# Experts stage: choices' transposes and sends two steps behind the scores, back half ten steps behind, norms one batch less ahead

## The chip, the cores and the metric

The kernel runs on one core of one Trainium2 chip. The metric is the device time of one execution in microseconds (us); lower is better. Engines are called PE (TensorE), DVE (VectorE), ACT (ScalarE), POOL (GpSimd) and SP (SyncE, which only issues DMAs here).

## The reference, cut to what matters

Two blocks (L0, L1) of attention and feed-forward run over x of 32 batches x 256 tokens x 128. The change touches the feed-forward of L0, a mixture of experts, and the modulated norm ahead of it:

```python
h = _layernorm(x, axis=-1) * (1 + cb) + sb
x = x + gb * _L0_ffn_ref(h, ...)

# _L0_ffn_ref: x (B, L, d); t = 32 experts, 4 sets, 32 hidden
grouped = x.reshape(B, g, t, d)                      # groups of 32 tokens
logits = jnp.einsum('bgtd,des->bgtes', grouped, controller)
logits = logits + tie
perm = (logits == jnp.max(logits, axis=-3, keepdims=True)).astype(x.dtype)
dispatched = jnp.einsum('bgtd,bgtes->bgesd', grouped, perm)
inner = jax.nn.relu(jnp.einsum('bgesd,desf->bgesf', dispatched, f1) + bias)
intermediate = jnp.einsum('bgesf,esfd->bgesd', inner, f2)
out = jnp.einsum('bgesd,bgtes->bgtd', intermediate, perm)
```

In each group of 32 tokens every pair of expert and set (128 slots) takes the token with the highest score, runs it through a small two-layer network, and hands the result back to that token.

## The kernel before

The stage is `experts_0`. Each engine has one program, written out by hand as a loop over steps i = 0, 1, 2, ...; engines meet through semaphores (`wait(engine, semaphore, count)`), and each engine takes its instructions strictly in the order written. So the place of a call in the loop of an engine is its place in the queue.

**Front half**, one batch n (256 tokens) at a time. DVE: `centre(n)` computes the statistics of X (L1345 stats, L1353 moments) and writes `centred` (L1359); POOL: `root(n)` turns the variance into `rstd` (L1302, L1306); DVE: `modulate(n)` writes `h` (L1369). PE: `turn(i)` transposes h of batch i into bank 0 (L1054), and into the other half of that bank the choice `takenT` of a former batch (L1060), and ACT copies both together to SBUF (`front_out`, L1238, tile `hT_taken`). PE: `score(i)` multiplies h by the controller and adds the tie row (L1071, L1072). DVE: `choose(i)` takes the maximum of each group (L1380, `best`) and compares (L1383, `takenT`). PE: `send` gathers the chosen tokens with the transposed choice (L1084; in the steps of `HALVED` it is two halves, L1099), and ACT copies them to the slots (`sent_out`, L1250).

**Back half**, a chunk m of 8 batches (`CB_` = 8) at a time, spread over eight steps s = 0 to 7; `back(i)` gives (m, s) from i - LAG. s = 0, 1: first matrices on PE (L1114), bias on DVE (L1390), relu on ACT (L1256). s = 2, 3: second matrices on PE (L1141), four rounds in a chunk, copied by DVE and ACT (`results_out`, L1221). s = 4 to 7 (`QUARTERS`): transposes back (L1153), copies (L1228), `hand_back` (L1165), `gate` on DVE (L1398, tile `delta`), residual on POOL (L1310). In steps LAG to 31 both halves run in the same step; the last chunk's back half runs without a front half.

**Sundries.** SP loads the modulation rows of a batch (L1020, tile `e_mod_norm`, four buffers), each load after the one before has landed and after h of the batch three earlier is written. Beside the stage, pieces of the last stage's weights are rounded on ACT (L1262), compared on POOL (L1315) and summed on ACT (L1267). `keep_busy` (L72) issues matmuls into an unused bank whose results nobody reads (filler).

In a step, PE's order is: `turn`, the odd `hand_back` of the step before, first or second matrices or two transposes back, `score`, `send`, then the rest of the back half with the even `hand_back`. ACT's order is: `front_out`, pieces, relu or copies, `sent_out`. DVE's order is: gate, bias or copies, `modulate`, `choose`, more copies, `centre`.

Of the kernel before, what the change touches and what calls it, by code (L numbers as in the profile page):

```python
# [23 lines left out]
P = 128  # L24
# [902 lines left out]
def experts_0(nc, ctx, dram, sbuf, psum, following):  # L927
# [56 lines left out]
    LAG = CB_ + 1  # L984
# [16 lines left out]
    HALVED = [i for i in range(STEPS) if front(i - 1) and back(i)[1] in (2, 3)]  # L1001
# [11 lines left out]
    with nc.Block() as block:  # L1013
# [33 lines left out]
        def _(pe):  # L1047
            def turn(i):
# [6 lines left out]
                if front(i - 1):  # L1055
                    if i >= LAG and back(i)[1] not in QUARTERS:
                        keep_busy(nc, B_TAKEN, sbuf["ident16"], 3)
                    wait(pe, takenT_done, i)
                    for t in range(TT):
                        last = nc.tensor.transpose(B_TAKEN[:, t * P:(t + 1) * P], takenT[:, (i - 1) % (2 * CB_), t * P:(t + 1) * P],  # L1060
                                                   ident[:, :])
# [26 lines left out]
            def send_half(i, half):  # L1088

                wait(pe, turned_done, i + 1)  # L1090
                wait(pe, sent_done, i - 1)
                if half == 1:
                    wait(pe, half_psum, HALVED.index(i) + 1)
                n = i - 1
# [23 lines left out]
            def second_matrices(i, m, r):  # L1118

                alone = m == NCHUNK - 1  # L1120
                if r == 0:
                    if alone:
                        keep_busy(nc, bank[4], sbuf["ident16"], 5)
                    wait(pe, sent_done, min(i - 1, B))
# [5 lines left out]
                if alone and r == 1:  # L1130
                    wait(pe, turned_done, B + 1)
# [40 lines left out]
            for i in range(STEPS):  # L1172
                m, s = back(i)
                before, at = back(i - 1)
                if i <= B:
                    turn(i)
# [26 lines left out]
                if front(i - 1) and i not in HALVED:  # L1203
                    send(i)
# [26 lines left out]
        def _(act):  # L1231
            def front_out(i):
# [3 lines left out]
                wait(act, sent_psum, i - 2)  # L1236
                part = slice(0 if front(i) else T, 2 * T if front(i - 1) else T)
                nc.scalar.copy(hT_taken[i % 2][:, part], bank[0][:, part]).then_inc(turned_done, 1)  # L1238

            def sent_out(n):  # L1240
# [3 lines left out]
                if n + 1 in HALVED:  # L1244
# [25 lines left out]
            def check_pieces(i):  # L1270
                if 0 <= i - PIECE_LAG - 2 < len(pieces):
                    sum_piece(i - PIECE_LAG - 2)
                if 0 <= i - PIECE_LAG - 1 < len(pieces):
                    round_piece(i - PIECE_LAG - 1)

            for i in range(STEPS):
                m, s = back(i)
                if i <= B:
                    front_out(i)
# [11 lines left out]
                if front(i - 1):  # L1291
                    sent_out(i - 1)
# [6 lines left out]
        def _(pool):  # L1299
# [18 lines left out]
            for n in range(3):  # L1318
                root(n)
            for i in range(STEPS):  # L1320
# [6 lines left out]
                if front(i + 3):  # L1327
                    root(i + 3)
# [7 lines left out]
                if 0 <= i - PIECE_LAG - 1 < len(pieces):  # L1336
                    compare_piece(i - PIECE_LAG - 1)

        @block.vector
        def _(dve):  # L1340
# [64 lines left out]
            for n in range(2):  # L1405
                modulate(n)
                centre(n + 1)
            for i in range(STEPS):
# [11 lines left out]
                if front(i + 2):  # L1420
# [1761 lines left out]
```

## Time and profile before

| | us |
|---|---|
| median of 3 runs | 1328.28 |
| lowest, highest | 1327.71, 1328.93 |
| the profiled execution, its own time | 1332.12 |
| its span in the profile | 1330.2 |
| mean granted clock of PE, share of full | 0.962 |

| engine | busy us | share of the span | instructions |
|---|---|---|---|
| PE, matmul | 1226.8 | 92% | 13717 |
| PE, weight load | 815.6 | 61% | 13717 |
| DVE | 1059.1 | 80% | 2967 |
| ACT | 931.9 | 70% | 1338 |
| POOL | 539.0 | 41% | 760 |

How to read it: these are averages over stages with different limits. The experts stage lies between about 408 and 632 us of the span; what a change in it is worth is read from its own steps. Times in the rows below are us from the start of the span.

### The profile page before, as it was taken

To read this page: it belongs to the slowest core of one execution; us is meant where nothing else is said; L and a number is where in the kernel's file an instruction comes from. 1 tells how busy PE (TensorE), PEld (TensorE's weight loads), DVE (VectorE), ACT (ScalarE), POOL (GpSimd) and SP (SyncE) were. 2 spreads that over 40 slices of the span, in tenths; PEclk is the share of its full clock that TensorE was granted. 3 is DMA by queue.
4 is the path that set the end of the run, shared out by engine and by line. 5 is a ranking of instruction groups with operands and counts; after the bars stand their busy time and mean duration, and the time that the engine had idled before them with its cause. 6 is when DMAs were issued, how large, how long until landed. Compare 5 with 4: busy or idle time off the path is not lost. (4 is left out here: it accounts for less than half of the span.)

```text
span 1330.2 us, 39845 instructions
## 1 busy us (share of the span) xinstructions
PE 1226.8 (92%) x13717; PEld 815.6 (61%) x13717; DVE 1059.1 (80%) x2967; ACT 931.9 (70%) x1338; POOL 539.0 (41%) x760
## 2 busy tenths in 40 slices
PE   3899999999996889998899999999879999999998
PEld 1555555555543667766455555555458878778776
DVE  4799999999965787756799999999646777777763
ACT  0588888888892556542588888788637676767665
POOL 2333333433421243422343343333236565656653
PEclk6699999999998999997899999999969999999999
DMA  4311111111001222100200000000000000000000
GB/s 119 136 36 36 35 35 35 35 35 35 28 10 48 59 50 63 53 19 2 104 14 16 13 12 16 12 12 16 6 2 9 9 16 8 16 8 16 11 12 25
DMA packets 47965, 40.69 MB, mean 31 GB/s; under 512 B 5376, under 2 KB 46688, under 8 KB 47360
## 3 DMA queue, kind: packets, MB, share of 16 engines
q1 hardware_dynamic: 47872, 39.45, 10.7%
q8 instruction: 58, 0.95, 0.3%
q14 instruction: 35, 0.29, 0.1%
HBM read 35.09 MB, written 4.34 MB: 30 GB/s over the span
## 5 line engine op out<-in xcount | busy, mean ns | idle before, releaser
L673 ACT ACTIVATE probs<-psum_all,biases 128x1024 f32<-128x1024 f32 x256 | 272.4, 1112 | 38.5 <-PE psum_all L581 37.5
L2393 ACT ACTIVATE a_probs<-psum_all 128x1024 f32<-128x1024 f32 x256 | 248.2, 1023 | 68.3 <-PE psum_all L2299 68.3
L2759 PE MATMUL psum_all<-ffn_hi,weights_r 128*128 128x512 f32 x704 | 285.3, 405 | 10.2 <-issue 4.2
L2759 PE MATMUL psum_all<-ffn_lo,weights_r 128*128 128x512 f32 x704 | 278.5, 396 | 0.0
L2719 POOL TENSOR_TENSOR ffn_lo<-ffn_full,ffn_hi 128x512 fp32r<-128x512 f32 x143 | 186.9, 1315 | 130.9 <-ACT ffn_hi L2836 95.2
L2759 PEld LDWEIGHTS psum_all<-ffn_hi,weights_r 128*128 128x128 f32 x704 | 134.2, 191 | 53.1 <-issue 11.3
L2759 PEld LDWEIGHTS psum_all<-ffn_lo,weights_r 128*128 128x128 f32 x704 | 134.6, 191 | 25.8
L594 PE MATMUL psum_all<-probs,vpad 128*32 128x257 f32 x2048 | 139.2, 389 | 0.3 <-ACT probs L673 0.3
L2313 PE MATMUL psum_all<-a_probs,vpad 128*32 128x256 f32 x2048 | 137.6, 386 | 0.0
L2848 ACT ACTIVATE ffn_full<-psum_all,scales 128x512 f32<-128x512 f32 x128 | 88.3, 690 | 67.8 <-PE psum_all L2759 67.7
L2719 DVE TENSOR_TENSOR ffn_lo<-ffn_full,ffn_hi 128x512 fp32r<-128x512 f32 x64 | 55.2, 862 | 79.5 <-ACT ffn_hi L2851 79.5
L402 POOL TENSOR_TENSOR a_vareps<-a_moments,eps 128x2 f32<-128x2 f32 x64 | 15.2, 238 | 185.3 <-DVE a_moments L439 185.3
L2851 ACT ACTIVATE ffn_hi<-psum_all,scales 128x512 fp32r<-128x512 f32 x128 | 87.4, 683 | 0.0
L594 PEld LDWEIGHTS psum_all<-probs,vpad 128*32 128x32 f32 x2048 | 53.8, 109 | 51.2 <-issue 21.4
L581 PE MATMUL psum_all<-a_qT,a_kT 32*128 32x256 f16 x1024 | 76.8, 276 | 8.6 <-ACT probs L673 7.3
L2313 PEld LDWEIGHTS psum_all<-a_probs,vpad 128*32 128x32 f32 x2048 | 53.6, 109 | 49.5 <-issue 27.6
L2089 POOL TENSOR_TENSOR a_vareps<-a_moments,eps 128x2 f32<-128x2 f32 x32 | 6.2, 194 | 180.2 <-DVE a_moments L2116 180.2
L2836 ACT CAST ffn_hi<-ffn_full 128x512 fp32r<-128x512 f32 x64 | 39.7, 620 | 43.2 <-DVE ffn_full L2918 43.2
L2299 PE MATMUL psum_all<-a_qT,a_kT 32*128 32x256 f16 x1024 | 65.6, 275 | 1.0 <-ACT a_probs L2393 0.9
L2913 DVE SCALAR_TENSOR_TENSOR ffn_gated<-ffn_tanh,psum_all 128x512 f32<-128x512 f32 x64 | 43.6, 681 | 12.1 <-ACT ffn_tanh L2842 12.1
L581 PEld LDWEIGHTS psum_all<-a_qT,a_kT 32*128 32x128 f16 x1024 | 23.8, 92 | 44.8 <-ACT probs L673 28.8
L2842 ACT ACTIVATE ffn_tanh<-psum_all,scales 128x512 f32<-128x512 f32 x64 | 43.5, 687 | 9.5 <-PE psum_all L2759 8.8
(231 smaller groups left out, 2655.2 us busy)
## 6 DMA issues: line engine op xcount, KB each, us to landing
a_mod_gate<-modulation_table SPq DMA_DIRECT2D x64, 128.0 KB, 2.9
X<-in_x SPq DMA_DIRECT2D x32, 128.0 KB, 2.9
a_mod_norm<-modulation_table SPq DMA_DIRECT2D x32, 128.0 KB, 3.0
f<-in_f SPq DMA_DIRECT2D x2, 2048.0 KB, 10.3
e_mod_norm<-modulation_table SPq DMA_DIRECT2D x32, 128.0 KB, 3.0
out<-X SPq DMA_DIRECT2D x16, 256.0 KB, 2.3
e_gates<-modulation_table SPq DMA_DIRECT2D x32, 64.0 KB, 2.8
weights<-in_h SPq DMA_DIRECT2D x2, 1024.0 KB, 7.6
```

Of the source, the lines that this page charges most:

```text
L581: last = nc.tensor.matmul(SC[c % 2][:, (TT * r + kb) * T:(TT * r + kb + 1) * T], kT[p][rows, g, kb * P:(kb + 1) * P], qT[p][rows, g, :], s ...
L594: last = nc.tensor.matmul(PO[32 * r:32 * r + 32, :], vpad[p][:, kb, G * r + g, :], probs[:, (2 * g + r // 2) % 4, r % 2, kb, 0:UNIT], star ...
L673: nc.scalar.activation(probs[:, c % 4, :, :, 0:T].rearrange("p r k q -> p (r k) q"), SC[c % 2].rearrange("p (a q) -> p a q", q=T), ACT.Tan ...
L2299: last = nc.tensor.matmul(SC[c % 2][:, (TT * r + kb) * T:(TT * r + kb + 1) * T], kT[p][rows, g, kb * P:(kb + 1) * P], qT[p][rows, g, :], s ...
L2313: last = nc.tensor.matmul(PO[32 * r:32 * r + 32, s * T:(s + 1) * T], vpad[p][:, kb, G * r + g, :], probs[:, (2 * g + r // 2) % 4, r % 2, k ...
L2393: nc.scalar.activation(probs[:, c % 4, :, :, :].rearrange("p r k q -> p (r k q)"), SC[c % 2], ACT.Exp, scale=float(np.float32(1.0) / np.sq ...
L2719: subtract(lo[layer][:, k, :], full[layer][:, k, :], hi[layer][:, k, :].bitcast(F32), ALU.subtract).then_inc(done[layer], 1)
L2759: ins = nc.tensor.matmul(dst, weights[:, w0:w0 + P], part[layer][:, k, :], start=first and i == 0, stop=last and i == len(parts) - 1)
L2842: nc.scalar.activation(tanh[:, m % 2, :], pair(m)[0], ACT.Tanh, scale=scales[:, 0, m:m + 1]).then_inc(tanh_done, 1)
L2848: nc.scalar.activation(full[layer + 1][:, m, :], bank[m % 2], ACT.Gelu, scale=scales[:, 1 + layer, m:m + 1]).then_inc(full_done[layer + 1], 1)
L2851: nc.scalar.activation(hi[layer + 1][:, m, :], bank[m % 2], ACT.Gelu, scale=scales[:, 1 + layer, m:m + 1]).then_inc(hi_done[layer + 1], 1)
L2913: nc.vector.scalar_tensor_tensor(out=gated[:, m % 2, :], in0=tanh[:, m % 2, :], scalar=1.0, in1=pair(m)[0], op0=ALU.add, op1=ALU.mult).the ...
```

## The change

The choice of batch n is now transposed and sent in step n + 2 instead of n + 1 (`front(i - 2)`, `n = i - 2`, `takenT_done` waited for at i - 1), so `turn` runs to step B + 1. `LAG` is 10 instead of 9: the back half of a chunk begins one step later, and there are 43 steps instead of 42. The filler of 3 matmuls ahead of the choice's transposes, which stood in the combined steps s = 0 to 3, is gone. `modulate` and `centre` stand one batch less ahead (`modulate(i + 1)`, `centre(i + 2)`, `root(i + 2)`), with one `modulate` and one `centre` less ahead of the loop. The pieces of weights are handled one step later. Weights, tiles, buffers and shapes are the same.

```diff
-    LAG = CB_ + 1
+    LAG = CB_ + 2
-    HALVED = [i for i in range(STEPS) if front(i - 1) and back(i)[1] in (2, 3)]
+    HALVED = [i for i in range(STEPS) if front(i - 2) and back(i)[1] in (2, 3)]
...
-                if front(i - 1):
-                    if i >= LAG and back(i)[1] not in QUARTERS:
-                        keep_busy(nc, B_TAKEN, sbuf["ident16"], 3)
-                    wait(pe, takenT_done, i)
+                if front(i - 2):
+                    wait(pe, takenT_done, i - 1)
                     for t in range(TT):
-                        last = nc.tensor.transpose(B_TAKEN[:, t * P:(t + 1) * P], takenT[:, (i - 1) % (2 * CB_), t * P:(t + 1) * P],
+                        last = nc.tensor.transpose(B_TAKEN[:, t * P:(t + 1) * P], takenT[:, (i - 2) % (2 * CB_), t * P:(t + 1) * P],
                                                    ident[:, :])
...
             def send(i):
                 wait(pe, turned_done, i + 1)
-                wait(pe, sent_done, i - 1)
+                wait(pe, sent_done, i - 2)
                 wait(pe, given_act, max(0, (i - LAG - 4) // CB_ + 1) * ROUNDS)
-                n = i - 1
+                n = i - 2
...
-                    wait(pe, sent_done, min(i - 1, B))
+                    wait(pe, sent_done, min(i - 2, B))
...
-                if i <= B:
+                if i <= B + 1:
                     turn(i)
...
-                wait(act, sent_psum, i - 2)
-                part = slice(0 if front(i) else T, 2 * T if front(i - 1) else T)
+                wait(act, sent_psum, i - 3)
+                part = slice(0 if front(i) else T, 2 * T if front(i - 2) else T)
...
-                if 0 <= i - PIECE_LAG - 2 < len(pieces):
-                    sum_piece(i - PIECE_LAG - 2)
-                if 0 <= i - PIECE_LAG - 1 < len(pieces):
-                    round_piece(i - PIECE_LAG - 1)
+                if 0 <= i - PIECE_LAG - 3 < len(pieces):
+                    sum_piece(i - PIECE_LAG - 3)
+                if 0 <= i - PIECE_LAG - 2 < len(pieces):
+                    round_piece(i - PIECE_LAG - 2)
...
-            for n in range(3):
+            for n in range(2):
                 root(n)
...
-                if front(i + 3):
-                    root(i + 3)
+                if front(i + 2):
+                    root(i + 2)
...
             centre(0)
-            for n in range(2):
-                modulate(n)
-                centre(n + 1)
+            modulate(0)
+            centre(1)
...
-                if front(i + 2):
-                    modulate(i + 2)
+                if front(i + 1):
+                    modulate(i + 1)
                 if front(i):
                     choose(i)
...
-                if front(i + 3):
-                    centre(i + 3)
+                if front(i + 2):
+                    centre(i + 2)
```

How it moves instructions. Lines of the changed kernel are two lower from L1071 on (L1069 is the score there, L1058 the choice's transposes, L1082 the send).

DVE at the start of the stage, up to the first choice, before (from the first `h`):

```order
413 L1369 SCALAR_TENSOR_TENSOR e_h<-e_centred,e_rstd,e_mod_norm 128x128 x2
414 L1345 BN_STATS e_stats<-X 128x6 x2
415 L1351 MEMSET e_unread 128x1
416 L1353 BN_AGGR e_moments<-e_stats 128x2 x2
417 L1359 SCALAR_TENSOR_TENSOR e_centred<-X,e_moments,e_mod_norm 128x128 x2
418 L1369 SCALAR_TENSOR_TENSOR e_h<-e_centred,e_rstd,e_mod_norm 128x128 x2
419 L1345 BN_STATS e_stats<-X 128x6 x2
420 L1351 MEMSET e_unread 128x1
421 L1353 BN_AGGR e_moments<-e_stats 128x2 x2
422 L1359 SCALAR_TENSOR_TENSOR e_centred<-X,e_moments,e_mod_norm 128x128 x2
423 L1369 SCALAR_TENSOR_TENSOR e_h<-e_centred,e_rstd,e_mod_norm 128x128 x2
424 L1380 TENSOR_REDUCE e_best<-psum_all 128x8
```

and changed:

```order
413 L1367 SCALAR_TENSOR_TENSOR e_h<-e_centred,e_rstd,e_mod_norm 128x128 x2
414 L1343 BN_STATS e_stats<-X 128x6 x2
415 L1349 MEMSET e_unread 128x1
416 L1351 BN_AGGR e_moments<-e_stats 128x2 x2
417 L1357 SCALAR_TENSOR_TENSOR e_centred<-X,e_moments,e_mod_norm 128x128 x2
418 L1367 SCALAR_TENSOR_TENSOR e_h<-e_centred,e_rstd,e_mod_norm 128x128 x2
419 L1378 TENSOR_REDUCE e_best<-psum_all 128x8
```

The first `best` moved ahead of the third batch's centring and h.

PE, the combined step s = 1 of the first chunk and the beginning of s = 2, before (two transposes of h, the filler, two transposes of the choice, then matrices):

```order
280 L1054 MATMUL psum_all<-ident,e_h 128x128 x2
281 L72 MATMUL psum_all<-ident 128x256 x3
282 L1060 MATMUL psum_all<-ident,e_takenT 128x128 x2
283 L1114 MATMUL psum_all<-e_slots,f 32x64 x64
284 L1071 MATMUL psum_all<-e_hT_taken,ctrl 128x256
285 L1072 MATMUL psum_all<-e_tie_parts,e_part_rows 128x256
286 L1084 MATMUL psum_all<-e_hT_taken,e_h 128x128 x8
287 L1054 MATMUL psum_all<-ident,e_h 128x128 x2
288 L72 MATMUL psum_all<-ident 128x256 x3
289 L1060 MATMUL psum_all<-ident,e_takenT 128x128 x2
290 L72 MATMUL psum_all<-ident 128x512 x2
291 L1141 MATMUL psum_all<-e_relued,f 128x64 x32
```

and changed:

```order
284 L1054 MATMUL psum_all<-ident,e_h 128x128 x2
285 L1058 MATMUL psum_all<-ident,e_takenT 128x128 x2
286 L1112 MATMUL psum_all<-e_slots,f 32x64 x64
287 L1069 MATMUL psum_all<-e_hT_taken,ctrl 128x256
288 L1070 MATMUL psum_all<-e_tie_parts,e_part_rows 128x256
289 L1082 MATMUL psum_all<-e_hT_taken,e_h 128x128 x8
290 L1054 MATMUL psum_all<-ident,e_h 128x128 x2
291 L1058 MATMUL psum_all<-ident,e_takenT 128x128 x2
292 L72 MATMUL psum_all<-ident 128x512 x2
293 L1139 MATMUL psum_all<-e_relued,f 128x64 x32
```

The filler ahead of the choice's transposes is gone; the one ahead of the second matrices stays.

PE, the end of the front half, step s = 6 of the third chunk, before:

```order
467 L1054 MATMUL psum_all<-ident,e_h 128x128 x2
468 L1060 MATMUL psum_all<-ident,e_takenT 128x128 x2
469 L1165 MATMUL psum_all<-e_givenT,e_takenT 32x128 x8
470 L1153 MATMUL psum_all<-ident,e_slots 128x128 x8
471 L1071 MATMUL psum_all<-e_hT_taken,ctrl 128x256
472 L1072 MATMUL psum_all<-e_tie_parts,e_part_rows 128x256
473 L1084 MATMUL psum_all<-e_hT_taken,e_h 128x128 x8
```

and changed:

```order
460 L1058 MATMUL psum_all<-ident,e_takenT 128x128 x2
461 L1163 MATMUL psum_all<-e_givenT,e_takenT 32x128 x8
462 L1151 MATMUL psum_all<-ident,e_slots 128x128 x8
463 L1082 MATMUL psum_all<-e_hT_taken,e_h 128x128 x8
```

The transposes of h and the score have left this step; transposes of a choice and a send are in it still.

## Rows read from the trace of the kernel before

**Rows 1.** Table by stretches: us, then busy us of each engine, PEclk, DMA share, GB/s.

```profile
412.30:600.00 187.70, 168.39 (x3284) 123.71 (x3288) 139.40 (x441) 100.97 (x228) 60.66 (x108) 0.99 0.20 51
600.00:613.70 13.70, 12.32 (x189) 12.13 (x186) 7.29 (x21) 4.54 (x9) 0.90 (x2) 0.50 0.01 2
```

**Rows 2.** Timeline, DVE, an opening step: start, us, operation, idle before and releaser.

```profile
434.98 0.61 DVE L1369 SCALAR_TENSOR_TENSOR e_h<-e_centred,e_rstd,e_mod_norm 128x128 f32<-128x128 f32 x2 [0.45 <-DVE e_centred L1359]
...
435.96 0.42 DVE L1383 TENSOR_TENSOR e_takenT<-psum_all,e_best 128x256 f32<-128x256 f32 x1
...
438.33 0.61 DVE L1369 SCALAR_TENSOR_TENSOR e_h<-e_centred,e_rstd,e_mod_norm 128x128 f32<-128x128 f32 x2 [0.45 <-DVE e_centred L1359]
```

**Rows 3.** Timeline, PE, the same opening step.

```profile
438.09 0.27 PE L1072 MATMUL psum_all<-e_tie_parts,e_part_rows 128*128 128x256 bf16 x1
```

**Rows 4.** Timeline, first chunk, s = 1 (DVE, ACT) and s = 2 (PE).

```profile
454.45 0.69 DVE L1390 TENSOR_TENSOR e_inner<-psum_all,ebias 128x512 f32<-128x512 f32 x1 [0.20 <-PE psum_all L1114]
...
454.55 0.42 ACT L1267 ACTIVATE e_piece<-e_piece 128x256 f32<-128x256 f32 x1 [1.41 <-POOL e_piece L1315]
...
457.41 0.60 PE L72 MATMUL psum_all<-ident 128*128 128x512 f16 x2 [0.47 <-ACT e_slots L1250]
```

**Rows 5.** Timeline, second chunk, the seam from s = 2 to s = 3.

```profile
513.74 2.01 PE L1141 MATMUL psum_all<-e_relued,f 32*128 32x64 f32 x64
...
512.39 1.29 DVE L1221 COPY e_slots<-psum_all 128x512 f32<-128x512 f32 x2 [0.82 <-PE psum_all L1141]
```

**Rows 6.** Timeline, PE, first chunk, score of a step in s = 4 to 7.

```profile
486.63 0.67 PE L1071 MATMUL psum_all<-e_hT_taken,ctrl 128*128 128x256 f32 x2 [0.20 <-DVE e_delta L1398]
```

**Rows 7.** Waits in 412 to 632 us: engine, line, waited for: us, times, longest.

```profile
PE psum_all L1060 <- DVE e_takenT L1383: 3.3, 9, 0.8
```

**Rows 8.** Timeline, PE, first matrices of the first chunk.

```profile
447.89 1.99 PE L1114 MATMUL psum_all<-e_slots,f 128*32 128x64 f32 x128 [0.16 <-ACT e_slots L1250]
```

**Rows 9.** Groups of instructions in 412 to 632 us, shapes apart: busy us, mean ns.

```profile
L72 PE MATMUL psum_all<-ident 128*128 128x256 f16 x48 | 8.2, 274 | 0.0
```

**Rows 10.** Timeline, second chunk, s = 0: h on DVE, the next transposes on PE.

```profile
500.14 0.44 PE L1054 MATMUL psum_all<-ident,e_h 128*128 128x128 f32 x2
...
499.49 0.60 DVE L1369 SCALAR_TENSOR_TENSOR e_h<-e_centred,e_rstd,e_mod_norm 128x128 f32<-128x128 f32 x2
```

**Rows 11.** Timeline, the start of the stage, in order of time.

```profile
413.20 0.37 ACT L1238 COPY e_hT_taken<-psum_all 128x256 f32<-128x256 f32 x1 [10.17 <-PE psum_all L1054]
...
414.86 3.21 PE L72 MATMUL psum_all<-ident 128*128 128x512 f16 x12
...
417.90 0.38 PE L1054 MATMUL psum_all<-ident,e_h 128*128 128x128 f32 x2
418.04 0.42 DVE L1380 TENSOR_REDUCE e_best<-psum_all 128x8 f32<-128x256 f32 x1
...
420.09 0.70 PE L1071 MATMUL psum_all<-e_hT_taken,ctrl 128*128 128x256 f32 x2 [0.46 <-ACT e_hT_taken L1238]
...
420.63 0.27 PE L1072 MATMUL psum_all<-e_tie_parts,e_part_rows 128*128 128x256 bf16 x1
...
424.28 0.61 DVE L1359 SCALAR_TENSOR_TENSOR e_centred<-X,e_moments,e_mod_norm 128x128 f32<-128x128 f32 x2 [1.07 <-issue]
...
424.93 0.61 DVE L1369 SCALAR_TENSOR_TENSOR e_h<-e_centred,e_rstd,e_mod_norm 128x128 f32<-128x128 f32 x2
```

**Rows 12.** Timeline, PE, third chunk, the odd hand backs of s = 5, 6, 7.

```profile
579.68 0.65 PE L1165 MATMUL psum_all<-e_givenT,e_takenT 128*32 128x128 f32 x16
...
584.80 0.64 PE L1165 MATMUL psum_all<-e_givenT,e_takenT 128*32 128x128 f32 x16 [0.28 <-issue]
...
589.37 0.65 PE L1165 MATMUL psum_all<-e_givenT,e_takenT 128*32 128x128 f32 x16 [0.65 <-DVE e_delta L1398]
```

**Rows 13.** Timeline, last chunk, second matrices on PE, a copy behind them on ACT.

```profile
597.62 11.70 PE L1141 MATMUL psum_all<-e_relued,f 32*128 32x64 f32 x252 [0.42 <-issue]
...
609.36 1.07 ACT L1221 COPY e_slots<-psum_all 128x512 f32<-128x512 f32 x2 [2.34 <-PE psum_all L1141]
```

More of the change, by code:

```diff
@@ L1090, in send_half @@
                 wait(pe, turned_done, i + 1)
-                wait(pe, sent_done, i - 1)
+                wait(pe, sent_done, i - 2)
                 if half == 1:
                     wait(pe, half_psum, HALVED.index(i) + 1)
-                n = i - 1
+                n = i - 2
                 for t in range(TT):
@@ L1130, in second_matrices @@
                 if alone and r == 1:
-                    wait(pe, turned_done, B + 1)
+                    wait(pe, turned_done, B + 2)
                     wait(pe, takenT_done, B)
@@ L1202, in _ @@
                     score(i)
-                if front(i - 1) and i not in HALVED:
+                if front(i - 2) and i not in HALVED:
                     send(i)
@@ L1243, in sent_out @@
                 wait(act, turned_back, (n // CB_ - 1) * TB_)
-                if n + 1 in HALVED:
+                if n + 2 in HALVED:
                     by_group = psum[:, 4 * 512:6 * 512].rearrange("p (b a t s) -> p t s a b", b=2, a=2, t=TT)
@@ L1270, in check_pieces @@
             def check_pieces(i):
+                if 0 <= i - PIECE_LAG - 3 < len(pieces):
+                    sum_piece(i - PIECE_LAG - 3)
                 if 0 <= i - PIECE_LAG - 2 < len(pieces):
-                    sum_piece(i - PIECE_LAG - 2)
-                if 0 <= i - PIECE_LAG - 1 < len(pieces):
-                    round_piece(i - PIECE_LAG - 1)
+                    round_piece(i - PIECE_LAG - 2)
             for i in range(STEPS):
                 m, s = back(i)
-                if i <= B:
+                if i <= B + 1:
                     front_out(i)
@@ L1290, in _ @@
                     results_out(act, nc.scalar.copy, given_act, m, 2 * (s - 2) + 1, 2)
-                if front(i - 1):
-                    sent_out(i - 1)
+                if front(i - 2):
+                    sent_out(i - 2)
                 if s in QUARTERS:
@@ L1335, in _ @@
                         following["rotate"](pool, 0)
-                if 0 <= i - PIECE_LAG - 1 < len(pieces):
-                    compare_piece(i - PIECE_LAG - 1)
+                if 0 <= i - PIECE_LAG - 2 < len(pieces):
+                    compare_piece(i - PIECE_LAG - 2)
         @block.vector
@@ L1452, in _ @@
                         following["rotated"](dve, 0)
-                if i == len(pieces) + PIECE_LAG + 2:
+                if i == len(pieces) + PIECE_LAG + 3:
                     wait(dve, piece_summed, len(pieces))
```

## Prediction

> **What bounds the kernel now.** I read the page first: the span is 1330.2 us, and the chain that ended last says nothing of the stage that is changed, the experts. So I cut that stage out with the table by stretches [rows 1]: from 412.3 to 600 us TensorE (PE) is busy 168 of 188 us, VectorE (DVE) 139. Neither is full, so each kind of step has to be read by itself in the timelines. I call them: opening steps (front half alone: transposes, scores, choice, send), combined steps s = 0 to 7 (front half of one batch and back half of the chunk before, s being the place in the chunk), and the last chunk, whose back half runs alone.
>
> *Opening steps.* One takes 3.35 us: h is written at 434.98 and the next one at 438.33 [rows 2]. Followed round: h, best and takenT on DVE, then the next batch's stats, moments, then vareps and rstd on GpSimd (POOL), and rstd lets DVE write the next h. From the start of takenT (435.96) to the next h (438.33) are 2.37 us, from h to takenT 0.98; together the whole 3.35. PE is not in this loop: the score's last matmul, with the tie row, ends at 438.09 + 0.27 = 438.36 [rows 3], and h, which stands ahead of best on DVE, ends at 438.33 + 0.61 = 438.94 [rows 2]. PE has 0.6 us of room.
>
> *Steps s = 0 and 1.* DVE is the closest to full. In s = 1 it waits for PE once, 0.20 us before the second bias [rows 4]. The other line is the ACT queue: moments (DVE), rstd and the comparison of a weight piece (POOL), which ACT waits for until 454.55; then the sum of that piece, its rounding, two relus and the copy of the slots, one behind the other. PE's second matrices wait for that copy: the filler in front of them starts at 457.41 after 0.47 us idle [rows 4].
>
> *Steps s = 2 and 3.* PE runs back to back, but at the seam to s = 3 the next second matrices (513.74) need the DVE copy that ends at 512.39 + 1.29 = 513.68 [rows 5]. They would start there whatever PE did before.
>
> *Steps s = 4 to 7.* PE is full but for 0.20 us before the scores, for a delta of DVE [rows 6].
>
> **The change, part by part.**
>
> *The wait for takenT.* The transposes of the choice of the step before become those of two steps before. What PE waited for takenT in the whole stage is one row: 3.3 us in 9 waits [rows 7]. Eight lie in opening steps, where the loop DVE-POOL-DVE sets the step (above): worth 0. The ninth is at the seam to the first combined step, and there the first matrices wait for ACT's copy of the slots anyway, 0.16 us more [rows 8]: worth 0.
>
> *The filler of 3 matmuls.* It goes in the 12 steps s = 0 to 3 of three chunks: 36 of the 48 of that shape, whose 8.2 us in 16 threes make 0.51 us each [rows 9]. What is late next, by step. In s = 0: PE could reach the next transposes of h at 500.14 - 0.51 = 499.63, but h of the next batch now is written in this very step (norms one batch less ahead), by 499.49 + 0.60 = 500.09 [rows 10]: a new wait of up to 0.5 us, and PE is where it was. Behind it on PE's queue stand the transposes of the choice and the first matrices of s = 1. In s = 1 these start about 0.5 us earlier, which spares DVE its wait of 0.20 us; h is then 0.2 us earlier. But s = 2 begins with ACT's copy, whose chain hangs on moments of s = 0 (unchanged): 0. In s = 3 the DVE copy ends last: 0. In s = 4 PE waits for DVE and ACT copies that follow its own second matrices: 0. So all 12 removals are worth 0 (between 0 and 12 x 0.51 = 6.1 us, were PE alone the bound; I take 0 because in s = 0, 2 and 3 a row shows another engine that ends within 0.1 us of PE's start).
>
> *The start of the stage.* Before the first step DVE now has two centrings and one h, instead of three and two. So the first choice comes about when the scores end, near 415 (the filler behind them starts at 414.86) instead of 418.04 [rows 11], and one more opening step has to fit in. The second choice now is bound by PE: the 12 filler matmuls in step 0 stand ahead of the transposes of h(1), which start at 417.90 as before; + 0.38, a copy of half width 0.37 with 0.09 of handing over, a score of 0.81 (420.09 to 420.90), 0.11: best of batch 1 at 419.66, takenT at 420.12. By the loop (2.37) h(3) follows at 422.49 and h(4), one turn of 3.35 later, at 425.84, where before h(4) stood at 424.93; the idle 1.07 us before the centring at 424.28 are used up. The profile puts them down to issue; I read them as its modulation rows, since each load waits for the one before [rows 11]. Sum: the extra opening step costs + 0.9 us. Bounds: 0 if the start hides it, + 3.35 if a whole step is added.
>
> *The end of the front half.* The last batch leaves the combined steps one step earlier relative to the back half: step s = 6 of the third chunk now has no transposes of h and no scores, as s = 7 has none now. Read from the starts of the odd hand back: with scores 584.80 - 579.68 = 5.12 us, without 589.37 - 584.80 = 4.57 us [rows 12]. Sum: - 0.55 us. The choices' transposes and the send stay in s = 6 and 7, and the first matrices of the last chunk wait for the same copy in the same place.
>
> *SP, POOL, pieces.* The load of modulation rows for batch n still waits for h(n - 3), which stands at the same distance ahead of the centring that reads it; the pieces of the weights move one step later with everything else. 0.
>
> *The sum.* 1332.12 (the profiled execution's own time) + 0.9 - 0.55 = 1332.5; the median of the three runs lies 3.84 us under that execution, so **1328.6 us**, own range 1327.0 to 1330.5.
>
> **The clock.** The filler that goes also kept PE at work. The granted clock is 0.99 as a mean to 600 us. From 600 it is 0.50 for 13.7 us, 2.4 us after the last chunk's second matrices began at 597.62 with nothing between their rounds, and through three more rounds [rows 1, 13]. Second matrices do not hold the clock by themselves. In steps s = 2 and 3 of the changed kernel there are the same rounds, four in a chunk, with idle stretches where the filler was, up to 0.47 + 0.51 = 1.0 us ahead of s = 2's. The Trainium skill, TensorE: Matmul & The Clock Gate, section "A second HAM failure mode: psum-queue depth-cycling", says that short idle times between groups of matmuls can be enough for the clock to go back and forth between its two levels; here the full clock did hold in s = 2 and 3, with the filler in, so no row shows what happens without it.
>
> **The rivals.**
>
> Clock lost (slower). Place: the second matrices in s = 2 or 3. A round takes 2.01 us at full clock [rows 5] and 3.41 at half (the copies behind it: 1.07 busy and 2.34 idle [rows 13]), so 1.4 us for each round run at half clock. One to two such rounds in each of three chunks are + 4.2 to + 8.4 us: 1333 to 1337. One chunk alone would stay under the 2.7 us that decide. For it: the fall at 600. Against: transposes, sends and scores stay between the rounds. Chance 0.20.
>
> PE was the bound after all (faster). If the removed filler comes off PE's path in most of the 12 steps, 0.3 to 0.51 each, - 3.6 to - 6.1 us: about 1324. For it: PE is busiest. Against: the seams above. Chance 0.10.
>
> The half-clock stretch moves (faster). The alone chunk loses about 1.4 us in each of three rounds. If the fall comes one round later or more, part of that goes: down by 1.4 to 4.2 us, 1324 to 1327. Nothing in the diff aims at it; the three runs agree within 1.2 us. Chance 0.08.
>
> The step does not shrink at the end and a whole opening step is added: + 3.35: 1331.6. Chance 0.04. The rest, 0.58, is my forecast.
>
> **How the numbers follow.** 0.2% (2.7 us) is about what a measurement of this kernel can tell from no change. My forecast (0.58) and a small part of the others lie within it: same 0.62. Faster: 0.10 and most of 0.08: 0.16. Slower: 0.20 and 0.02: 0.22. The range leaves out the lower half of the PE case and the upper half of the clock case: 1325.0 to 1333.5.
>
> **What would show it.** Right: first choice near 415, the second near 419.7; opening steps still 3.35 us; PE waiting for h in s = 0 and for ACT's copy in s = 2 longer than 0.47 us; the clock at 1.00 up to the last chunk; the stage's end within 1 us of 632. Wrong: combined steps s = 0 to 3 shorter than before by 0.3 us or more each (PE case), or a clock under 1 in s = 2 or 3.

## The result and the profile after

The changed kernel takes 1348.97 us as a median of four runs (1336.04 to 1354.69), the kernel before beside it 1328.61 (1327.71 to 1329.66): a ratio of 1.0142, 95% interval 1.0116 to 1.0168. It is slower, by 1.4%, and its runs lie 19 us apart where those of before lie 2 us apart. The profiled execution of the changed kernel took 1345.75 us, with a span of 1343.9 us against 1330.2. Ten more runs of the same changed kernel, further down (again), have their median at 1339.03 us, a ratio of 1.0073, so how much is lost differs from one set of runs to the next. In two comparisons further down the slowest runs were set aside when the ratio was made (one of twelve of taken_late; three of ten of fill_s3, its profiled one among them); since the spread is itself the effect here, medians below are those of all runs.

The answer to [rows 1], for the changed kernel. Table by stretches, TensorE alone: stretch, us, busy us (count), granted clock, DMA share, GB/s.

```profile
410.90:508.60 97.70, 82.76 (x1471) 0.97 0.22 57
508.60:532.50 23.90, 23.90 (x285) 0.50 0.23 41
532.50:563.20 30.70, 28.21 (x578) 1.00 0.20 56
563.20:590.50 27.30, 27.30 (x323) 0.50 0.08 22
590.50:624.60 34.10, 30.17 (x779) 1.00 0.08 19
624.60:628.00 3.40, 3.02 (x14) 0.51 0.00 0
628.00:646.00 18.00, 13.21 (x190) 1.00 0.01 2
```

Before, the clock was at half once in this stage behind its first microseconds, for 13.7 us in the last chunk. Now it is at half for 23.9 us in the second chunk and for 27.3 us in the third, and for 3.4 us in the last. TensorE is busy for 100% of both long stretches: a full engine, at half speed.

Where the first fall stands. Timeline of the changed kernel, PE, second chunk, s = 2 and the seam to s = 3 (start, us, operation, idle before and releaser).

```profile
504.76 0.41 PE L1054 MATMUL psum_all<-ident,e_h 128*128 128x128 f32 x2
505.00 0.38 PE L1058 MATMUL psum_all<-ident,e_takenT 128*128 128x128 f32 x2
506.86 0.60 PE L72 MATMUL psum_all<-ident 128*128 128x512 f16 x2 [1.48 <-ACT e_slots L1248]
507.40 2.62 PE L1139 MATMUL psum_all<-e_relued,f 32*128 32x64 f32 x64
...
512.48 3.69 PE L1139 MATMUL psum_all<-e_relued,f 32*128 32x64 f32 x64
```

This is the place of [rows 4] and [rows 5]. The idle piece ahead of the second matrices was 0.47 us and is now 1.48 in this chunk (1.32 in the first, 1.48 in the third). 1.2 us into the first round behind it the clock falls (508.6); the round takes 2.62 us and the next one 3.69, where [rows 5] has 2.01. In the third chunk it falls sooner, within the filler and before any second matrices (it is 1.00 until 563.2 and 0.57 as a mean from 563.2 to 563.5):

```profile
563.02 0.85 PE L72 MATMUL psum_all<-ident 128*128 128x512 f16 x2 [1.48 <-ACT e_slots L1248]
563.80 3.69 PE L1139 MATMUL psum_all<-e_relued,f 32*128 32x64 f32 x64
```

In the second chunk it rises only here, in s = 4:

```profile
529.77 1.91 PE L1151 MATMUL psum_all<-ident,e_slots 128*128 128x128 f32 x8
531.48 1.07 PE L1069 MATMUL psum_all<-e_hT_taken,ctrl 128*128 128x256 f32 x2
532.34 0.37 PE L1070 MATMUL psum_all<-e_tie_parts,e_part_rows 128*128 128x256 bf16 x1
```

But for the first 1.2 us, all four rounds of second matrices (32 rows of TensorE each), and everything between them, ran at half clock.

The cost by chunk is read from ACT's copies of the transposes, one in each step. The first combined step's copy starts 0.69 us later than before (448.45 against 447.76), the one at the end of the first chunk's steps 0.70 later (491.15 against 490.45). Over the second chunk the delay grows to 8.08 (562.86 against 554.78), over the third to 18.20 (602.75 against 584.55). The last chunk, whose own half-clock stretch is 10.3 us shorter, gives 3.9 back: from the last of these copies to DVE's last copy of the chunk's results it takes 39.26 us (602.75 to 642.01), before 43.16 (584.55 to 627.71). 18.20 - 3.9 = 14.3, close to the 13.7 by which the span is longer.

### The profile page after: what moved, and what is told of

Same layout as the page of the kernel before. It is cut to its first block and busy times, and to the rows that moved or that the text cites. A ratio compares the mean times of both kernels' runs of the same rounds, so it can differ in the third digit from the quotient of the medians.

```text
span 1343.9 us, 39780 instructions
## 1 busy us (share of the span) xinstructions
PE 1241.3 (92%) x13683; PEld 828.4 (62%) x13683; DVE 1058.6 (79%) x2967; ACT 933.3 (69%) x1339; POOL 539.2 (40%) x760
## 5 line engine op out<-in xcount | busy, mean ns | idle before, releaser
L2756 PEld LDWEIGHTS psum_all<-ffn_hi,weights_r 128*128 128x128 f32 x704 | 134.4, 191 | 51.8 <-DVE ffn_full L2915 10.3
L1300 POOL TENSOR_TENSOR e_vareps<-e_moments,eps 128x2 f32<-128x2 f32 x32 | 6.2, 195 | 113.2 <-DVE e_moments L1351 112.7
## 6 DMA issues: line engine op xcount, KB each, us to landing
f<-in_f SPq DMA_DIRECT2D x2, 2048.0 KB, 10.3
```

The lines of the kernel that those rows point to most:

```text
L2756: ins = nc.tensor.matmul(dst, weights[:, w0:w0 + P], part[layer][:, k, :], start=first and i == 0, stop=last and i == len(parts) - 1)
```

## Experiments

A chunk is said to lose the clock if its second matrices run at half clock in the profiled execution. "Idle" is TensorE's idle time between the transposes of s = 2 and the filler ahead of its second matrices.

**1. The filler back in the changed kernel (fill_back), and out of the kernel before (fill_out_before).**

```diff
 fill_back: the changed kernel
+                    if i >= LAG and back(i)[1] not in QUARTERS:
+                        keep_busy(nc, B_TAKEN, sbuf["ident16"], 3)
 fill_out_before: the kernel before
-                    if i >= LAG and back(i)[1] not in QUARTERS:
-                        keep_busy(nc, B_TAKEN, sbuf["ident16"], 3)
```

> The changed kernel with the filler of 3 matmuls put back ahead of the choice's transposes in s = 0 to 3. Clock theory (the filler kept the clock at 1.00 through the second matrices): 1327 to 1330 us, clock 1.00 in the second and third chunk, spread of the runs under 3 us. Rival (the new order itself, its lag and the norms one batch less ahead, cost the time): stays at 1340 to 1350 us.

> The kernel before with this filler taken out and nothing else changed. Clock theory: 1335 to 1355 us, uneven from run to run, clock at 0.50 in the second matrices of one or more chunks. Rival (order): 1328 us. If the wait for takenT, which the filler covered, is what keeps it safe: also 1328 us.

Measured: fill_back 1331.79 us (7 runs), ratio 1.0039 (1.0014 to 1.0065); fill_out_before 1326.76 (10 runs), ratio 0.9996 (0.9975 to 1.0017), both against 1328.26. Neither loses the clock in a chunk. fill_back came out above its 1327 to 1330 us, and its runs lie 9 us apart (1329.77 to 1338.73), not under 3; of the three cases for fill_out_before the last one came, that the wait for takenT keeps it safe. So in the old order the filler is worth nothing, as predicted. In the new order the kernel with the filler is 3.5 us slower than the kernel before, and about 4 us slower than the new order that keeps its clock without it (fill_gap, below): there the filler does cost time. Its profile has 3.4 us at half clock about 445 us, in the last opening step, but fill_gap (1327.68 us) has one as long there, 446.3 to 449.7, so that is not the reason. Only both together cost 0.7 to 1.4%: early transposes of the choice, and no filler. The timeline of fill_out_before, PE, same place, shows the difference:

```profile
504.11 0.44 PE L1058 MATMUL psum_all<-ident,e_takenT 128*128 128x128 f32 x2 [0.36 <-DVE e_takenT L1381]
505.03 0.60 PE L72 MATMUL psum_all<-ident 128*128 128x512 f16 x2 [0.48 <-ACT e_slots L1248]
```

There TensorE still waits 0.36 us for takenT, as it does in s = 1, and reaches the wait for ACT later. Idle ahead of the second matrices: 0.84 us in two pieces.

**2. The filler in one of the steps alone (fill_s2, fill_s3).** The same two lines, with `if back(i)[1] == 2:` or `== 3:`.

> The changed kernel with the filler only in s = 2. Place theory A (the idle 1.3 to 1.5 us ahead of the second matrices is where the clock is lost): 1328 to 1331 us. Place theory B (the filler between the rounds, s = 3, is what counts): 1340 to 1350 us.

> The changed kernel with the filler only in s = 3. Theory A: 1340 to 1350 us, the clock falls behind the idle time ahead of s = 2's matrices as in the changed kernel. Theory B: 1328 to 1331 us.

Measured: fill_s2 1329.47 us (1326.47 to 1340.45, 10 runs), ratio 1.0024 (1.0002 to 1.0046), no chunk lost in the profiled execution (the run of 1340.45, at a mean clock of 0.952, may have lost one). fill_s3 1341.45 us (1326.20 to 1354.94, 10 runs), ratio 1.0049 (1.0013 to 1.0085) without its three slowest; first and second chunk lost. Timeline of fill_s3, PE, first chunk:

```profile
457.19 0.61 PE L72 MATMUL psum_all<-ident 128*128 128x512 f16 x2 [1.46 <-ACT e_slots L1250]
457.72 3.05 PE L1141 MATMUL psum_all<-e_relued,f 32*128 32x64 f32 x64
```

The same filler helps if it stands in s = 2 alone and does not help in s = 3 alone. The place is the idle ahead of the first round. A filler in s = 3 also does not bring the clock back.

**3. What about the place counts (taken_late, fill_32, fill_gap).** Three edits of the changed kernel, none with the old filler.

```diff
 taken_late
-                    wait(pe, takenT_done, i - 1)
+                    wait(pe, takenT_done, min(i, B))
 fill_32, ahead of the transposes of the choice
+                    if i >= LAG and back(i)[1] not in QUARTERS:
+                        rows = sbuf["ident16"][0:NF, :]
+                        for _ in range(3):
+                            nc.tensor.matmul(B_TAKEN, rows, rows.unsqueeze(1).broadcast_to([NF, B_TAKEN.shape[1] // P, P]), start=True, stop=True)
 fill_gap, behind the transposes of the choice
+                if s == 2:
+                    wait(pe, inner_done, m * ROUNDS + 3)
+                    keep_busy(nc, bank[2], sbuf["ident16"], 2)
```

> The changed kernel without any filler, with one more wait: the choice's transposes of each step wait for the newest choice, as in the kernel before, though they no longer use it. That puts the idle time of TensorE back ahead of the choice's transposes, so that they stand between it and the second matrices, and splits the one idle piece of about 1.4 us. Theory A (the idle piece just ahead of the 32-row second matrices loses the clock; in one piece it does, in two it doesn't): about 1327 to 1331 us, granted clock 1.00 in the second matrices of the first three chunks, the idle time shown as one of 0.3 to 0.5 us on takenT and one of about 0.5 us on the ACT copy. Theory B (full-row work of the filler itself is needed wherever the back half stands one step later): as changed, 1336 to 1355 us with 24 us at half clock in one or more of the chunks.

> The changed kernel with the removed filler back in its four places of each chunk, of the same columns (three matmuls of 256), but on 32 of the 128 rows of TensorE. It fills the same time with another kind of work. Theory A (what counts is how long TensorE is idle in one piece ahead of the second matrices): as with the full filler, about 1329 to 1333 us, clock 1.00 in the second matrices. Theory C (what counts is how much work on all 128 rows stands there; work on 32 rows counts as idle): the clock falls as in the changed kernel, 1336 to 1355 us, with stretches of 24 to 27 us at half clock that begin in the second matrices.

> The changed kernel with a filler of two matmuls of 512 columns on all rows put inside the idle piece: behind the choice's transposes of the third combined step of each chunk and ahead of the wait for the ACT copy (and none elsewhere). It runs while TensorE would be idle. Theories A and C agree: the clock holds at 1.00 through the second matrices of the first three chunks, the idle piece is 0.7 to 1.1 us instead of 1.3 to 1.5, and the time is 1326 to 1331 us, no more than with the filler ahead of the choice's transposes. If what matters is instead the distance between the last full-row transposes and the second matrices in the place of the old filler, the clock falls here: 1336 us or more.

Measured, 12 runs each against 1327.68: taken_late 1328.16, ratio 1.0002 (0.9981 to 1.0023), one run of 1483.73 at a mean clock of 0.739 among them, which nothing here explains (the others end at 1332.60); fill_32 1331.82, ratio 1.0030 (1.0012 to 1.0049); fill_gap 1327.68 (1325.07 to 1328.97), ratio 0.9993 (0.9974 to 1.0012). None loses the clock in a chunk. First taken_late, then fill_32, then fill_gap, PE, the wait ahead of s = 2's second matrices in the second chunk:

```profile
505.36 0.44 PE L1058 MATMUL psum_all<-ident,e_takenT 128*128 128x128 f32 x2 [0.29 <-DVE e_takenT L1381]
506.29 0.60 PE L72 MATMUL psum_all<-ident 128*128 128x512 f16 x2 [0.49 <-ACT e_slots L1248]
```

```profile
508.05 0.60 PE L72 MATMUL psum_all<-ident 128*128 128x512 f16 x2 [0.35 <-ACT e_slots L1252]
```

```profile
507.39 0.60 PE L72 MATMUL psum_all<-ident 128*128 128x512 f16 x2 [1.04 <-ACT e_slots L1251]
```

A wait alone, which adds no work at all, takes the whole loss away: the filler's work isn't needed (theory B falls). With filler on 32 rows the clock stays up as with filler on 128 rows, and it costs the same (1331.82 against 1331.79). That fits theory A, but it does not refute theory C, that 32-row work counts as idle at this place: the filler there takes 0.50 us and the idle left is 0.35, together 0.85, and so much idle lost the clock in no chunk (see 5). The filler in the gap costs nothing, since TensorE would be idle, and its twelve runs lie within 3.9 us.

**4. One piece or the sum (split_gap).** taken_late splits the idle and also shortens it. This edit splits it nearly alone:

```diff
+                if s == 2:
+                    wait(pe, relued_done, (m + 1) * ROUNDS)
+                    keep_busy(nc, bank[2][:, 0:P], sbuf["ident16"], 1)
```

> The changed kernel with one matmul of 128 columns on all rows (under 0.1 us of work) put into the idle piece ahead of the third combined step's second matrices, behind the last relu of the chunk, which ends about the middle of the piece. The idle time stays nearly what it was (about 1.2 us in all), in two pieces of about 0.5 and 0.7 us. The runs so far don't separate the length of one piece from the sum of idle time: where the clock held, both were smaller. If the length of one piece decides, the clock holds at 1.00 in the first three chunks in all runs and the times lie together at 1326 to 1330 us. If the sum of idle time (or the little full-row work) ahead of the 32-row rounds decides, it falls in one or more chunks from run to run as in the changed kernel, and the times spread over 1333 to 1347 us.

Measured: 1335.65 us (1328.18 to 1346.79, 10 runs), ratio 1.0082 (1.0051 to 1.0112). The first chunk was lost, behind these waits (timeline, PE):

```profile
457.24 0.23 PE L72 MATMUL psum_all<-ident 128*128 128x128 f16 x1 [0.36 <-ACT e_relued L1257]
458.19 0.61 PE L72 MATMUL psum_all<-ident 128*128 128x512 f16 x2 [0.72 <-ACT e_slots L1251]
458.73 2.49 PE L1139 MATMUL psum_all<-e_relued,f 32*128 32x64 f32 x64
```

My theory A, that the length of one piece decides, falls in this form. Two pieces of 0.36 and 0.72 us lose the clock too, and one of 1.04 (fill_gap) did not. The sum of the idle time there fits better, but it isn't shown to be what decides: 1.08 and 1.04 lie close together, the second and third chunk of split_gap kept the clock with sums of 1.25 and 1.24, and fill_gap also has more full-row work in the place.

**5. The changed kernel again, unaltered (again).**

> The changed kernel once more, unaltered, on the chip of the two runs beside it and in more rounds, to see how its time spreads. If the idle piece of 1.3 to 1.5 us ahead of the second matrices makes the clock fall in some of the three chunks and not in others from run to run, the times lie between about 1328 (no chunk) and 1355 us (three chunks), wide apart, with the mean granted clock falling as the time rises, about 7 to 9 us for each chunk that loses it. If it falls in the same chunks each time, they lie within 3 us of one another.

Measured: 1339.03 us (1333.01 to 1346.94, 10 runs), against 1328.11, ratio 1.0073 (1.0042 to 1.0103). Mean clocks run from 0.947 (1346.94) to 0.959 (1333.01), time falling on the whole as the clock rises. In the profiled run only the third chunk was lost. Timeline, PE, second chunk and then third:

```profile
505.45 0.60 PE L72 MATMUL psum_all<-ident 128*128 128x512 f16 x2 [1.47 <-ACT e_slots L1248]
505.98 2.01 PE L1139 MATMUL psum_all<-e_relued,f 32*128 32x64 f32 x64
...
555.98 0.61 PE L72 MATMUL psum_all<-ident 128*128 128x512 f16 x2 [1.47 <-ACT e_slots L1248]
556.51 3.00 PE L1139 MATMUL psum_all<-e_relued,f 32*128 32x64 f32 x64
```

The same idle of 1.47 us, ahead of the same work, once kept and once lost the clock. Idle time there makes a loss possible, not certain. I counted all chunks whose idle I read in the profiles of all fourteen kernels: where it summed to 1.08 us or more, 8 of 14 lost the clock; where it summed to less (0 to 1.05), none of 28 did. That is a count, not a limit of the chip. What decides in a given chunk is open; the rows of PE just ahead of the two above are alike.

**6. What brings the clock back (long_fill).**

```diff
                 if i in HALVED:
-                    keep_busy(nc, B_OUT, sbuf["ident16"], 2)
+                    keep_busy(nc, B_OUT, sbuf["ident16"], 26 if back(i)[1] == 3 else 2)
```

> The changed kernel, with 24 more matmuls of 256 columns on all 128 rows in the fourth combined step of each chunk, between the two rounds of second matrices there, ahead of the score. At full clock they take about 2.7 us, at half 5.2. Theory D (a clock that fell in the third combined step stays down as long as the work is mostly 32-row rounds, and comes back behind a few us of full-row work in a row): where a chunk loses the clock at its second matrices, the stretch at half clock is no longer 24 to 27 us but ends within or just behind the added filler, some 13 to 18 us after it began. Theory E (the stretch has a length of its own, whatever runs): 24 to 27 us as before. Either way the time is not less than the changed kernel's by much: each chunk pays 2.7 to 5.2 us for the filler and gives back up to 5: 1336 to 1355 us.

Measured: 1347.23 us (1338.10 to 1353.81, 6 runs), ratio 1.0129 (1.0089 to 1.0170). Two chunks lost, each with 17.1 us at half clock instead of 23.9 or 27.3. Timeline of long_fill, PE, first chunk, s = 3:

```profile
469.10 3.69 PE L1139 MATMUL psum_all<-e_relued,f 32*128 32x64 f32 x64
472.56 1.17 PE L1097 MATMUL psum_all<-e_hT_taken,e_h 32*128 32x128 f32 x8
473.67 3.96 PE L72 MATMUL psum_all<-ident 128*128 128x256 f16 x26
477.47 0.60 PE L1069 MATMUL psum_all<-e_hT_taken,ctrl 128*128 128x256 f32 x2
...
478.10 2.01 PE L1139 MATMUL psum_all<-e_relued,f 32*128 32x64 f32 x64
```

```profile
463.00:475.50 12.50, 12.50 (x159) 0.50 0.08 22
475.50:480.00 4.50, 4.50 (x88) 0.98 0.02 4
```

The table by stretches below it has the clock at 0.50 and then 0.98: it rose within the added filler, and the last round behind it took 2.01 us again. Theory D fits and theory E falls: the half-clock stretch has no fixed length, it ended within full-row work in a row. In the changed kernel as much of it in a row comes only in s = 4. The filler is paid in every chunk, lost or not: 1347.23 us against 1339.03 of the unaltered kernel beside it (again), so this is no remedy.

**7. Two attempts at a faster kernel (tail_fill, start_4).** tail_fill is the kernel before with filler between the rounds of the last chunk; start_4 is fill_gap with the filler of the first opening step cut.

```diff
 tail_fill
                 wait(pe, relued_done, m * ROUNDS + (r + 1))
+                if alone:
+                    keep_busy(nc, second_banks(m, r)[0], sbuf["ident16"], 2)
 start_4
-                    keep_busy(nc, bank[2], sbuf["ident16"], 1 if i else 12)
+                    keep_busy(nc, bank[2], sbuf["ident16"], 1 if i else 4)
```

> The kernel before with a filler of two matmuls of 512 columns on all rows ahead of each of the four rounds of second matrices of the last chunk, into a bank that the round then overwrites. Before, the last chunk's rounds run for 13.7 us at half clock (four rounds in 11.70 us). Theory C (32-row work back to back loses the clock, full-row work between keeps it): the clock stays at 1.00 to the end of the stage, four rounds take about 8 us plus 4 x 0.4 us of filler, and the time falls by 1 to 4 us to 1324 to 1327 us. If the copies of the rounds bound the end of the stage, the clock holds but the time is the same, 1328; if the clock falls there for another reason, the filler only adds: 1330 us.

> The changed kernel with the filler in the idle piece (as in the run that held the clock) and the filler of the first opening step cut from 12 matmuls of 512 columns to 4. The second score waits behind those 12, and VectorE waits for it for 1.2 to 2.1 us. If the opening steps then keep their pace, the stage ends about 1.2 to 1.8 us earlier than with the 12: about 1326 us, 0.999 of the kernel before, which 5 rounds may just not tell from 1. If the filler is what brings the clock up at the start, the clock rises later, the opening steps take longer, and the time is the same or up to 3 us more.

Measured: tail_fill 1328.77 us (12 runs), ratio 0.9999 (0.9978 to 1.0021); start_4 1328.65 (12 runs), ratio 1.0007 (0.9985 to 1.0029). Neither beats the kernel before: for tail_fill the second of its three cases came, for start_4 not the 1326 us expected. In tail_fill the rounds of the last chunk run at full clock, but they do so without this filler too in the profiled executions of fill_out_before, fill_gap and the changed kernel, so nothing shows that the filler did it. TensorE then waits for a copy, and the clock falls behind that wait for 3.4 us (timeline, PE, then the table by stretches):

```profile
604.34 2.01 PE L1143 MATMUL psum_all<-e_relued,f 32*128 32x64 f32 x64
607.76 1.50 PE L1155 MATMUL psum_all<-ident,e_slots 128*128 128x128 f32 x8 [1.41 <-DVE e_slots L1223]
```

```profile
596.00:608.00 12.00, 10.59 (x267) 1.00 0.02 4
608.00:611.00 3.00, 3.00 (x18) 0.55 0.03 5
```

Behind this wait of 1.41 us stand full-row transposes, and the clock is back after 3.4 us; behind the 1.48 us in s = 2 stand the rounds, and it was 23.9.

In start_4 the second choice is 1.1 us earlier after the first copy than in fill_gap (418.10 - 412.61 against 419.36 - 412.76), the clock still rises, and the first combined step comes 1.08 us earlier after it (34.79 us against 35.87; 0.84 earlier than in taken_late). In the second chunk's s = 4 ACT waits a little longer for a piece of the weights (start_4, then fill_gap, timeline, ACT):

```profile
524.57 0.40 ACT L1263 CAST e_piece_r<-e_piece 128x256 fp32r<-128x256 f32 x1 [1.19 <-DMA e_piece<-in_h]
```

```profile
525.66 0.41 ACT L1263 CAST e_piece_r<-e_piece 128x256 fp32r<-128x256 f32 x1 [0.98 <-DMA e_piece<-in_h]
```

That is 0.2 us of what was won. Most of the rest goes in the last chunk: from the last copy of the transposes to DVE's last copy of the results it takes 39.65 us (583.56 to 623.21), in fill_gap 38.91 (584.65 to 623.56). Why is not shown. No version here beats the kernel before by more than a measurement tells; fill_gap equals it with the changed order.

## Why the prediction was wrong

**What held.** The steps in which the clock stayed up went as forecast. From the first combined step of the first chunk to its end the copies keep their distance, 42.70 us (448.45 to 491.15) against 42.69 before: four fillers less, worth 0. fill_out_before says the same of the whole kernel in the old order. Most opening steps still take 3.35 us. Of the two waits that I named one came, for ACT's copy in s = 2, longer than 0.47 us. At the end of the front half (ACT's copies, changed kernel):

```profile
598.18 0.37 ACT L1236 COPY e_hT_taken<-psum_all 128x256 f32<-128x256 f32 x1 [0.36 <-PE psum_all L1058]
...
602.75 0.37 ACT L1236 COPY e_hT_taken<-psum_all 128x256 f32<-128x256 f32 x1 [0.36 <-PE psum_all L1058]
```

are 4.57 us apart, the figure of [rows 12], so the - 0.55 was right. With the clock held (taken_late 1328.16, fill_gap 1327.68 us) the whole is where the sum of 1328.6 had it, so the rivals of a bound PE, of an added opening step and of a step that doesn't shrink are out.

**What did not hold, and cost nothing.** The other wait that I named, for h in s = 0, did not come. The changed kernel's waits for h (412 to 640 us: us, times, longest) are

```profile
PE psum_all L1054 <- DVE e_h L1367: 2.9, 8, 0.7
```

and all eight lie in opening steps, the last at 447.30. In the second chunk's s = 0, h is written by 500.00 + 0.61 = 500.61 and its transposes start at 500.75 without a wait; from one step's transposes to the next it is 4.57 us (496.18 to 500.75), before 4.67 (495.47 to 500.14), so the step did not shrink by the filler's 0.51 either. What took up the rest is open. And "all 12 removals are worth 0" holds for the old order only: from the first combined step's copy to the last copy it takes 137.23 us in fill_back (448.65 to 585.88), 136.02 in fill_gap (448.63 to 584.65) and 135.25 in taken_late (447.90 to 583.15).

**The start of the stage**, + 0.9 forecast, was mis-sized in the profiled run. From the first copy to the one of the first combined step it is 36.65 us (411.80 to 448.45), before 34.56 (413.20 to 447.76): + 2.09. Against [rows 11] (changed kernel, start of the stage):

```profile
413.45 4.25 PE L72 MATMUL psum_all<-ident 128*128 128x512 f16 x12
...
413.72 0.42 DVE L1378 TENSOR_REDUCE e_best<-psum_all 128x8 f32<-128x256 f32 x1
...
419.30 0.42 DVE L1378 TENSOR_REDUCE e_best<-psum_all 128x8 f32<-128x256 f32 x1 [2.13 <-PE psum_all L1070]
```

The 12 fillers took 4.25 us where [rows 11] has 3.21, because the clock rose later in them. 1.04 of the 1.2 us missing is this. In again, the same kernel, it rose earlier in them,

```profile
413.19 3.13 PE L72 MATMUL psum_all<-ident 128*128 128x512 f16 x12
```

and the stretch is 35.50 us (411.54 to 447.04): + 0.94, the forecast. So this term was right but for the clock.

**The step that failed: the clock.** The forecast put the loss of the clock at nothing. The loss and its place were named, as a rival with a chance of 0.20; two terms of that rival were wrong, and so was the reading under it.

First, the idle. I put it at "up to 0.47 + 0.51 = 1.0 us" ahead of s = 2's second matrices, taking off the filler of s = 2 alone. But where an engine waits for another that doesn't come earlier, what is saved in the step ahead piles up at the same wait: s = 1's filler of 0.51 us goes there too. 0.47 + 0.51 + 0.51 = 1.49; measured 1.48. I had written that in s = 1 things "start about 0.5 us earlier" and stopped there. With the wait for takenT kept, as in fill_out_before, a part of it would have been taken up ahead of the choice's transposes. So I valued the removed wait at 0 in time, rightly, and did not ask what idle it had kept apart from the second matrices. Against the clock case I argued that "transposes, sends and scores stay between the rounds"; they stayed, and the clock fell in the first round in the second chunk, and ahead of it in the third.

Second, the price. I took 1.4 us for each of one or two rounds in a chunk, though the stretch of [rows 13] ran on through three more, until the last chunk's transposes followed. I did not ask what brings the clock back. In the combined steps nothing does until s = 4: four rounds and the work between them, 23.9 to 27.3 us. Instead of 4.2 to 8.4 us for three chunks it is 7.4 us for the second chunk (8.08 - 0.70) and 10.1 for the third (18.20 - 8.08). One to three chunks lost at that price fit the times of again and of the first four runs; only profiled executions show how many were lost.

Third, the reading. From [rows 13] I took it that "second matrices do not hold the clock by themselves". In the last chunk of fill_out_before (timeline, PE) all 256 of them run back to back,

```profile
595.46 7.80 PE L1139 MATMUL psum_all<-e_relued,f 32*128 32x64 f32 x256
```

at a granted clock of 1.00 throughout. What the runs tie the fall in s = 2 to is the idle time ahead of the rounds, not the rounds. Why the last chunk of the kernel before lost the clock is open.

The Trainium skill, TensorE: Matmul & The Clock Gate, section "A second HAM failure mode: psum-queue depth-cycling", which the prediction weighed, speaks of frequent short idle times between groups of matmuls, with which the clock goes back and forth. The trace agrees in kind: idle of 1.48 us ahead of a group, then the fall, though here one such place in a chunk was enough. It was read as a doubt when it should have raised the chance, since the change removed both the filler and the wait that had kept that idle short.

The half-clock stretch of the last chunk did get shorter, as one rival had it, and gave back 3.9 us, hidden under the 18.2 lost.

## What to carry to other kernels

Price the removal of a filler or of a wait twice: once in time, where it may be worth 0, and once in idle time, summed over the steps that end at the same wait, and look at what kind of work stands behind that wait. If the clock can fall there, ask where it would rise again, since most of the price is that distance. And where one engine must wait anyway, put the filler inside that wait: in fill_gap it cost nothing and made the runs the most even of all.

## What the runs showed of the hardware

- TensorE was busy for 100% of 23.9 and of 27.3 us at half clock, and the clock did not rise. The work was rounds of small matmuls (32 rows of weights, 64 columns, 3.69 us a round) with shorter pieces on all rows between them. 26 matmuls of filler on all rows in a row (3.96 us, long_fill) brought it up before they ended. Yet the small rounds alone did not lower a clock that was up: 7.80 us of them back to back ran at 1.00 (fill_out_before).
- In the changed kernel's third chunk the clock fell in the filler behind 1.48 us of idle, before the small matmuls had begun. But the same idle of 1.47 us ahead of the same rounds lost the clock in one chunk and not in another of one execution. So one kernel's times spread: 1333.0 to 1346.9 us in ten runs. A single profile of such a kernel says little; the mean granted clock of each run (0.947 to 0.959) sorts them.
- The kernel before has such a place too, in the last chunk: half clock for 13.7 us in its profiled execution, while in that of fill_out_before (span 1321.9) the clock is 0.99 as a mean from 420 to 630 us. In the largest comparison its own runs lie between 1324.48 and 1336.25 us (35 runs), not within 2 us. I did not find an edit that removes this for good.
